# Order and number of filler matmuls in TensorE's queue for the first two tiles of an attention and expert layer

## What is computed

```python
q, k, v = sigmoid(x@Wq+bq), sigmoid(x@Wk+bk), x@Wv+bv          # 16 heads of 8
sink_in = n / sum(q * cumsum(k)); src_out = n / sum(k * cumsum(q))
cons_sink = sum(q * cumsum(k*src_out)) / n
cons_src  = clip(sum(k * cumsum(q*sink_in)) / n, -1, 1)
e = exp(cons_src); vs = v * e / cumsum(e) * n
kv = cumsum(outer(k, vs))                                       # 8 x 8 per head and token
att = (q*sink_in/n) . kv * sigmoid(cons_sink)
h = ln(x + att@Wo + bo); h2 = ln(h + gelu(h@W1+b1)@W2 + b2); x2 = ln(x + h2)
logits = x2@gate_w.T + gate_b                                   # softmax, best two of 8 experts
expert_e(x2) = relu(x2@wi.T + bi + x2@A_e.T@B_e.T) @ wo.T + bo
out = ln(x2 + sum of the two chosen experts * gate)
```

## Time and profile before

| what | value |
| --- | --- |
| median of 3 runs | 397.83 us |
| the profiled execution | 398.05 us, its span 396.2 us |
| TensorE matmul / weight load | 365.0 us (92%) / 257.5 us (65%) |
| VectorE | 331.0 us (84%) |
| GpSimd | 254.8 us (64%) |
| ScalarE | 214.0 us (54%) |
| DMA | 26.59 MB, mean 67 GB/s |
| granted TensorE clock, mean | 0.996 of full speed |

### The profile page before, as it was taken

The page is one execution under the profiler, slowest core; times in us unless marked ns, Lnnn a source line. Parts: engine busy times, 40 slices in busy tenths (PEclk is TensorE's granted clock), DMA queues, the critical chain, the costliest instruction groups (busy, mean ns, idle before and its releaser), DMA issues. The chain is left out here.

```text
span 396.2 us, 6691 instructions
## 1 busy us (share of the span) xinstructions
PE 365.0 (92%) x2050; PEld 257.5 (65%) x2050; DVE 331.0 (84%) x799; ACT 214.0 (54%) x396; POOL 254.8 (64%) x431
## 2 busy tenths in 40 slices
PE   8988989898989999899999999899999997999992
PEld 3555765865749675777568675778477664955652
DVE  2789999978688979998899979997999989844543
ACT  3331418245572796268832885188734883286450
POOL 2034759887499459982898449963898469955231
PEclk9999999999999999999999999999999999999998
DMA  8509046008200029000740047001810054000001
GB/s 250 195 2 208 4 96 172 2 1 185 81 0 2 0 55 230 12 0 2 182 109 2 2 98 196 2 1 23 204 42 1 0 133 107 2 0 29 0 20 34
DMA packets 19875, 26.59 MB, mean 67 GB/s; under 512 B 1664, under 2 KB 9984, under 8 KB 19840
## 3 DMA queue, kind: packets, MB, share of 16 engines
q1 hardware_dynamic: 19696, 25.96, 25.7%
q10 hardware_dynamic: 144, 0.21, 0.2%
HBM read 7.29 MB, written 2.10 MB: 24 GB/s over the span
## 5 line engine op out<-in xcount | busy, mean ns | idle before, releaser
L1034 POOL TENSOR_TENSOR prod<-cum_kv,q_fac 128x512 f32<-128x512 f32 x64 | 93.5, 1478 | 17.0 <-DVE cum_kv L1271 11.5
L458 PEld LDWEIGHTS pO<-s_wor,prod 128*128 128x128 f32 x512 | 63.0, 191 | 20.1 <-issue 12.0
L458 PE MATMUL pO<-s_wor,prod 128*128 128x128 f32 x512 | 67.3, 278 | 4.8 <-POOL prod L1034 4.8
L1265 DVE TENSOR_TENSOR kv<-k,vb 128x512 f32<-128x512 f32 x64 | 53.0, 830 | 1.1 <-DMA vb<-vs 1.0
L1021 POOL TENSOR_TENSOR var_eps<-mv,s_con 128x4 f32<-128x4 f32 x32 | 7.2, 224 | 60.2 <-DVE mv L1293 60.2
L1271 DVE TENSOR_TENSOR_SCAN cum_kv<-p_ones,cum_kv,kv 128x512 f32<-128x512 f32 x32 | 40.6, 1278 | 0.6
L1271 DVE TENSOR_TENSOR_SCAN cum_kv<-p_ones,kv 128x512 f32<-128x512 f32 x32 | 38.8, 1218 | 0.7
L479 PE MATMUL pG<-hT,s_ffn 128*128 128x512 f32 x64 | 31.1, 608 | 2.4 <-ACT hT L858 1.5
L1024 POOL TENSOR_TENSOR rstd<-var_eps,s_con 128x4 f32<-128x4 f32 x32 | 33.0, 1030 | 0.0
L486 PE MATMUL pY<-s_ffn,gel 128*128 128x128 f32 x256 | 32.4, 276 | 0.0
L486 PEld LDWEIGHTS pY<-s_ffn,gel 128*128 128x128 f32 x256 | 30.6, 192 | 1.4 <-issue 0.7
(11 more groups left out here) (199 smaller groups left out, 835.5 us busy)
## 6 DMA issues: line engine op xcount, KB each, us to landing
vb<-vs SPq DMA_DIRECT2D x64, 256.0 KB, 4.6
xT<-x_t SPq DMA_DIRECT2D x8, 256.0 KB, 3.9
xt<-x SPq DMA_DIRECT2D x8, 256.0 KB, 5.2
out<-y SPq DMA_DIRECT2D x7, 256.0 KB, 2.3
s_moe<-moe_w SPq DMA_DIRECT2D x1, 836.0 KB, 10.0
s_wor<-wo_rep SPq DMA_DIRECT2D x1, 512.0 KB, 7.9
s_ffn<-ffn_w SPq DMA_DIRECT2D x1, 512.0 KB, 8.4
s_con<-consts SPq DMA_DIRECT2D x1, 502.0 KB, 4.6
```

Of the source, the lines that this page charges most:

```text
L458: mm = pe.matmul(pO3[:, s, :], prod[:, m % 4, s * P:(s + 1) * P], s_wor[:, m, :], start=False, stop=(m == DH - 1), skip_group_check=True)
L1034: pool.tensor_tensor(prod[:, m % 4, :], cum_kv[t.par][:, m, :], q_fac[t.par][:, :], ALU.mult).then_inc(prod_ready, 1)
L1265: dve.tensor_tensor(kv[:, m % 3, :], k[t.par][:, :], vb[:, m, :], ALU.mult).then_inc(kv_ready, 1)
```

## The change

Only the order of calls and the number of fillers in TensorE's queue change; other engines' lists, the data and all buffers stay. In `second_step`, `reduce_out(b, 6)` goes ahead of `compensation_T(a)` and `factor_T(a)`. In `third_step` one of two fillers before `h_T(c)` and the filler between `h_T(c)` and `hidden(c, 0)` go; later `reduce_out(b, 3)` and `reduce_out(b, 4)` go ahead of both `head_sums(a, 1, ...)`, and between `reduce_out(b, 2)` and `reduce_out(b, 5)` there are six fillers in place of three.

```diff
@@ second_step, TensorE
                 keep_busy(1)
                 reduce_out(b, 5)
                 keep_busy(1)
+                reduce_out(b, 6)
                 compensation_T(a); factor_T(a)
-                reduce_out(b, 6)
                 keep_busy(1)
                 reduce_out(b, 7)
@@ third_step, TensorE
                 project_v(a)
                 keep_busy(1)
                 head_sums(a, 0, True); head_sums(a, 0, False)
-                keep_busy(2)
+                keep_busy(1)
                 pe.wait_ge(y_free[1], 16)
-                h_T(c)
-                keep_busy(1, pG[1])
-                hidden(c, 0); hidden(c, 1)
+                h_T(c); hidden(c, 0); hidden(c, 1)
                 hidden(c, 2); hidden(c, 3)
                 denominators_T(a, 0); denominators_T(a, 1)
                 ffn_out(c, 0)
...
                 reduce_out(b, 1)
                 ffn_out(c, 2); ffn_out(c, 3)
                 reduce_out(b, 2)
+                keep_busy(1, pM)
+                reduce_out(b, 3)
+                keep_busy(2, pM)
+                reduce_out(b, 4)
+                keep_busy(1, pM)
                 head_sums(a, 1, True)
-                reduce_out(b, 3)
                 keep_busy(1, pM)
-                reduce_out(b, 4)
                 head_sums(a, 1, False)
-                keep_busy(2, pM)
+                keep_busy(1, pM)
                 reduce_out(b, 5)
                 keep_busy(1, pM)
                 cumulate_e(a)
```

## The result

The changed kernel takes 401.4 us (median of 7 runs, 399.36 to 401.94), the kernel before 397.7 us (median of 7): ratio 1.0081, 95% interval 1.0057 to 1.0104. Forecast was 400.6 us, range 398.4 to 402.4. The sign and the place were right, and the moves did nearly what was worked out; but the median holds one thing that the forecast had as an unlikely rival, a fall of TensorE's clock in about half of the executions.

A forecast was written before the change was run, and what follows sets the result against it. TensorE (92% busy) and VectorE (84%) were taken to work nearly all the time, bound by in-order queues and hand-overs. Profiled 398.05 + 1.0 + 0 + 1.8 = 400.85, less 0.22, gave 400.6 us; range 398.4 to 402.4.

The forecast's parts named there:

- The sign "clock 1.00": Around `h_T` in the third step: TensorE idle on both sides of it, yet its granted clock still 1.00.
- Move 1: Second step, `reduce_out(0,6)` ahead of the transposes: `vs` 1.7 us later, tile 0's statistics 1.0 us later.
- VectorE's larger lag: After move 1 VectorE lags 1.7 us, 0.7 more than TensorE; this goes in its 1.03 + 2.08 us wait before `cons`.
- Move 2: Third step, reductions 3 and 4 ahead of both head sums: these and `cons` 2.08 us late, tile 1's statistics 1.8.
- The fillers around `h_T(0)`: Third step: taking two fillers out, before `h_T(0)` and between it and `hidden`, yields 0; other bound 1.72 us gained.
- Rival 3: TensorE's clock falls around 61 to 64 us, at `hidden`: 3.9 us more, 404.5 us; chance 0.06.
- Rival 1: Delay given back at TensorE's later 1.77 us wait for ScalarE's `x`: only +1.0, 398.8 us; chance 0.14.
- Rival 2: Move 1 covered by VectorE's 0.63 us and small gaps around ScalarE's `n`; move 2 stays: +1.8, 399.6; chance 0.06.
- Rival 4: Faster: fillers at `h_T(0)` were last to end, so taking two out gives 1.72, 396.1 us; chance 0.08.
- Sum: Whole kernel: 1.0 + 0 + 1.8 us on the profiled 398.05, 400.85; 0.22 above the median, hence 400.6 us.

The follow-up runs named there:

- both_moves: The changed kernel with the two fillers around `h_T(0)` put back as before; 400.12 us, ratio 1.0067.
- move1: The kernel before with only `reduce_out(0,6)` ahead of the second step's transposes; 398.16 us, ratio 1.0023.
- move2: The kernel before with only reductions 3 and 4 of tile 1 ahead of both head sums and three fillers more; 399.10 us, ratio 1.0038.
- fillers_out: The kernel before with only the two fillers around `h_T(0)` taken out; 397.88 us, ratio 1.0013.
- all_fillers_out: The kernel before with all three fillers around `h_T(0)` taken out; 398.34 us, ratio 1.0022.

## Why the prediction was right, and where not

The signs that the prediction named for the moves can be read in both_moves, which has no fall. Put on the time of the kernel before (add 43.55), `cons` is at 83.51 (forecast 83.6) and the statistics of tile 1 at 92.38 (forecast 92.6), with the end +2.62. The sign "clock 1.00" around `h_T` held there, and failed in all three profiles of the changed kernel.

- *Move 1, 1.0 us.* Right in mechanism and size: in move1 `vs` +1.63 (forecast 1.7), statistics of tile 0 +0.95, end +0.91.
- *VectorE's larger lag goes before `cons`.* Right: in both_moves `cons` is +3.02, where move1 has +0.92 and move2 +2.09, and the wait there is 2 us longer. The moves add: end +2.62 for both, 0.91 + 1.65 = 2.56 one by one.
- *Move 2, 1.8 us.* Right in mechanism, mis-sized by 0.2. The second head sums and `cons` came 2.09 later, forecast 2.08. But `x` came only 1.76 later, not 2.08, and `x2_T` 1.58, not 1.8. Of the missing 0.32 at `x`, 0.22 is VectorE's `kv` behind `cons`, which took 0.66 us where it had taken 0.88 (rows of move2 above). Why is not shown: GpSimd was at work beside it both times, with `e_norm` before and with product 6 in move2. The step that failed is that everything behind `cons` keeps its duration.
- *The fillers around `h_T(0)`, 0 us.* Right for what they hold up (fillers_out, table), wrong in effect. That step was "taking two out yields 0". Their cost was in the clock: 1.32 to 1.50 us at the transposes after `hidden` in all three profiles of the changed kernel, and part of its times: 4 of 7 in the first set and 3 of 6 in the second lie between 401.3 and 402, which carries the median of the first set to 401.4.
- *Rival 3, the fall of the clock.* Given 0.06 and 3.9 us more. It happened in about half of the executions and cost 1.3 to 1.5. Its price was too high because the clock was back after 3.4 us, before the transposes, which ran at full pace: 3.4 us at half rate lose 1.7, and from `hidden` to the transposes 5.23, 5.40 and 5.34 us were measured for 3.89, so 1.34 to 1.51. The rest went into the 0.45 us that this stretch had spent waiting (3.89 us less four matmuls of 0.86). Its chance was too low because one stretch with a single wait of 1.77 us was taken to speak for a stretch with two waits around 0.44 us of transposes; and the transposes at its end start at 118.90, so that only the last 0.1 us of the stretch was transposes. The Trainium skill (TensorE: Matmul & The Clock Gate, Part 4: PE-mode transpose) says that in transpose mode the clock gate's full rate does not engage, as a transpose does not count as busy in the same way. No run here replaces the transposes by ordinary matmuls, so that they count less is not shown; what the runs show is that with a filler of ordinary matmuls on either side of them none of ten fell.
- *Rivals 1, 2 and 4* fell: nothing is given back (the wait at `x2_T(1)` is 1.77 before and after), move 1 is not covered, the fillers were not in the way.
- *Sum.* 2.8 forecast; 2.62 from the moves in the trace, and 3.7 in the medians of the first set with the falls. Moves alone are 400.12 us, 0.5 below the forecast, and the median with the falls is 0.8 above it. That the forecast lies between the two is luck: the range went up to 402.4 for later steps that fall less well, while the fall of the clock, which brought 401.4, stood outside it at 404.5.

Open: most of the lower group of the changed kernel, 399.4 to 399.8, is 2 us below the upper one and below the fastest of the fifteen runs with either or both fillers kept (399.80), while a fall costs 1.2 to 1.5 in the traces. Part can be the start of the span (1.1 us between profiles). No profile of that group was got, so the rest has no explanation here.

## What to carry to other kernels

A filler that never delays anything may still do work: before taking one out, look at what stands idle on both sides of it, and time enough executions to see two groups; where each execution comes with its mean granted clock, that tells at once whether the groups part by the clock. Lay the queue out from start to start and follow the engine that waits for the late item: the cost of a late hand-over is the delay less the slack behind it, and a hand-over on which two chains meet costs when late and gives nothing when early. Compare traces from a common event inside the kernel, not from the start of the span.

## What the runs showed of the hardware that was not expected

The granted clock fell to half for 3.4 us (65.2 to 68.7) in a kernel that is 92% busy on TensorE, with waits of 1.04 and 1.09 us and 0.44 us of transposes between them; and by the mean clock it did so in 19 of 33 executions of one program. With one filler of 0.86 us on either side it fell in none of ten. With a wait of 1.90 us before the transposes and 1.09 behind (all_fillers_out) the one profile taken has no fall, and by the mean clock six of eleven executions fell.

From the first projection to the next, two matmul records, it took between 0.96 us (both_moves) and 1.83 us (the changed kernel), with a clock column of 1.00 in either case, and the whole execution shifts by it: the event at 42.73 to 43.80 us moves mostly with this pace and not with the landing of the weights.
